# A post-norm transformer block: the transposed inputs of later batches made by DMAs and POOL, or by TensorE

## The chip, the core and the metric

The kernel runs on one core of one Trainium2 chip. The metric is the device time of one execution in microseconds (us). "Before" is the kernel as found; the profile of it is one further execution.

## The reference

Four batches of 512 tokens with 512 features go through attention (16 heads of 32, causal), a residual and a layer norm, then through a gated feed-forward layer with integer weights, a residual and a layer norm, all in float32. Cut to what matters:

```python
qkv = x @ w_qkv.T + b_qkv                    # x: (4, 512, 512), w_qkv: (1536, 512)
p = softmax(q @ k.T / sqrt(32) + causal)
x = layernorm(x + (p @ v) @ w_out.T + b_out)
g = x @ ((gate_w - 128) * gate_scale).T      # gate_w, up_w: (2048, 512), down_w: (512, 2048)
u = x @ ((up_w - 128) * up_scale).T
x = layernorm(x + (silu(g) * u) @ ((down_w - 128) * down_scale).T)
```

## The kernel before

**Engines and order.** Every engine's program is written out by hand and runs in its own order; semaphores join them. TensorE multiplies, ScalarE (ACT) and VectorE (DVE) empty the banks and split operands, GpSimd (POOL) and SyncE (SP) issue DMAs, and POOL does small vector work. An instruction that waits holds up all behind it on its engine.

**Attention.** The work goes in 16 groups: batch b has groups 4b to 4b+3, each with four heads. A group has 16 steps, and tables say what is done in which step: SCORE_STEPS, MAX_STEPS, EXP_STEPS, TASK_STEPS (transposes of probs through `ident`, L1296), and `filling`, which spreads projections between them. Every product of activations and weights is made of three matmuls from operands split into a high and a low part (xT_hi and xT_lo, wT_hi and wT_lo). The projections of group G+2 (L1220) stand in group G, so those of the next batch begin in step 8 of the group with g = 2.

**The transposed x.** A projection needs x with features on the partitions. Before, for batch b+1 SP loads x_tok (tokens on partitions, `load_x_ahead`, L518; y1 of batch 0 comes as the fourth such input, L521), TensorE transposes it in group 4b+2, steps 1, 2, 5 and 6 (X_STEPS; X_FIRST in group 2), four 128x128 transposes a step into one bank (`transpose_x`, L1192), ScalarE rounds the bank to xT_hi (`x_hi`, L750), and DVE takes the rest to xT_lo (`x_lo`, L952).

**Feed-forward.** Per batch 16 blocks i: `gate_up` makes 16 matmuls (L1438, L1439), ScalarE silu (L865), DVE hid (L1089), and `down` 8 matmuls (L1445, L1446). The weights are widened from shorter copies on the way: POOL's DMAs write 16-bit copies to DRAM during the attention (`shorten`), SP fetches them by transposing DMAs in four chunks (`load_short`, L545 to L551, 12 DMAs a chunk), and ScalarE widens them piece by piece in batch 0 (`widen_piece`, L828 and L833). If the weights' values didn't fit, a second path would read them through w_int instead; POOL issues the 48 loads of w_int (L722) in either case, each after the one two before it has landed. The input of batches 1 to 3 comes from y1_dram: SP loads x_tok, TensorE transposes it (L1405; in batch 0 as the last pieces of blocks 12 to 15, in batches 1 and 2 as turns between blocks, TURNS), ScalarE copies the banks to yT_next (L859, L922) and splits it (`y_hi`, L878), and DVE takes the low part (`y_lo`, L1098).

**POOL's order before.** Per group: `att_lo`, `widen_inverse` (a copy of 512 elements, L658), in some groups the layer norm's `apply_norm` (L645) and `add_bias`; after the attention the last `apply_norm`, then the 48 loads of w_int, then `root` for batches 0 to 2.

Of the kernel before, what the change touches and what calls it, by code (L numbers as in the profile page):

```python
# [6 lines left out]
def postln_block_kernel(nc: bass.Bass, x, w_qkv, b_qkv, w_out, b_out, gate_w, gate_scale, up_w, up_scale,  # L7
# [10 lines left out]
    BF16 = mybir.dt.bfloat16  # L18
# [49 lines left out]
    X_FIRST = [2, 4, 5, 6]  # L68
# [49 lines left out]
    def x_at(G, s):  # L118
        return [t for t in range(NT) if (X_STEPS if G > NG else X_FIRST)[t] == s] if G % NG == 2 else []

# [49 lines left out]
    for G, (jobs, counts) in enumerate(FILLING):  # L170
        for s in range(STEPS):
# [6 lines left out]
            for t in x_at(G, s):  # L178
                banks.whole(("x", G // NG + 1, t))
# [15 lines left out]
    down_short = nc.dram_tensor("down_short", (D, I), BF16, kind="Internal").ap()  # L195
    x_v = x.rearrange("b (t p) d -> b p t d", p=P)
# [14 lines left out]
    def pieces_at(i, short=False):  # L211
# [4 lines left out]
        if r == NI // TPR:  # L216
            return first + ahead + [("y", t)]
# [5 lines left out]
    WEIGHTS = [p for p in PIECES if p[0] != "y"]  # L223

    SHORT_PIECES = FIRST_PIECES + [p for i in range(NI) for p in pieces_at(i, True)]
    SHORT_WEIGHTS = [p for p in SHORT_PIECES if p[0] != "y"]
# [10 lines left out]
    TURNS = list(range(9)) + [("y", 0)] + list(range(9, 12)) + [("y", 2)] + list(range(12, NI))  # L237

# [5 lines left out]

    def of_batch(view, b):
        return view[bass.ds(b, 1)].rearrange("o p t d -> (o p) t d")

    ctx = ExitStack()
    with ctx:
# [9 lines left out]
        xT_hi = sb("xT_hi", [P, ND, S], F32R)  # L259
        xT_lo = sb("xT_lo", [P, ND, S], F32R)  # L260
# [104 lines left out]
        x_loaded = sem("x_loaded")  # L365
# [33 lines left out]
        yT_kept = sem("yT_kept")  # L399
        y_loaded = sem("y_loaded")  # L400
        r_loaded = sem("r_loaded")
        yT_full = sem("yT_full")
# [25 lines left out]
        def turns_of(ahead):  # L428
            return TURNS if ahead else list(range(NI))

        def piece_place(piece, weights):
# [7 lines left out]
            if kind == "d":  # L439
                return downT[:, TPR * n:TPR * (n + 1), piece[2] * P:(piece[2] + 1) * P]  # L440
            return yT_next[:, n, :].rearrange("p (t q) -> p t q", t=NT)
# [11 lines left out]
        def full_by(n, weights):  # L453

            return n + 1 if weights is wide_weights else sum(piece[0] == "y" for piece in PIECES[:n + 1])

        def piece_evicted(piece, order=WEIGHTS):

            if piece[0] == "y":
                return yT_kept, piece[1] + 1  # L460
            return fw_placed, order.index(piece) + 1
# [19 lines left out]
        def residual(b):  # L481
            return scan_buf if b == LAST else z_tok

# [3 lines left out]
        def _(sp):  # L487
# [25 lines left out]
            def load_x_ahead(b):  # L513

                for t in range(NT):
                    wait_full(sp, "x", b - 1, t)
# [1062 lines left out]
```

## Time and profile before

| | us |
|---|---|
| runs of the kernel before | 748.05, 748.51, 752.32 |
| median | 748.51 |
| the profiled execution | 748.73 |
| its span in the profile | 746.8 |
| TensorE busy | 724.9 (97%) |
| DVE, ScalarE, POOL busy | 393.5, 379.6, 135.4 |

The profile shows one execution. Matmuls overlap, so a line's mean duration is longer than the step from one start to the next; what a matmul costs in the queue is read from starts in the timeline. The first 383 us are the attention, the rest the feed-forward part, whose batches 1 and 2 take 88.8 us each.

### The profile page before, as it was taken

The page shows a single profiled execution, that of the slowest core. Times are in us where ns is not written, and L with a number is a line of the kernel's source. Part 1 is how long each engine was busy: PE and PEld are TensorE (multiplying, and loading weights), DVE is VectorE, ACT ScalarE, POOL GpSimd, SP SyncE. Part 2 cuts the span into 40 slices and gives each one's busy share as a digit, 9 for nine tenths or more (in the row PEclk, how much of TensorE's full clock was granted, in tenths as well). Part 3 has the DMA queues.
Part 4 walks back from the last instruction along what each step waited for, and adds up shares of the span by engine and source line. Part 5 has one row for each costly group of instructions (what it writes and reads, how often), then busy time and mean ns, then how long its engine had stood idle before and what let it go on. Part 6 is the DMA issues. An engine that isn't in the chain of part 4 may idle for free.

```text
span 746.8 us, 11957 instructions
## 1 busy us (share of the span) xinstructions
PE 724.9 (97%) x4480; PEld 564.2 (76%) x4480; DVE 393.5 (53%) x1004; ACT 379.6 (51%) x912; POOL 135.4 (18%) x154
## 2 busy tenths in 40 slices
PE   7998899999999999999899999999999999999994
PEld 6776677777777767777688888888888888888883
DVE  4766766666667665676652222643236332463335
ACT  3665866766866666866766554322232223322230
POOL 0010110305222151413724222220000000000004
PEclk9999999999999999999999999999999999999998
DMA  9201523335531465212577964431210020000201
GB/s 315 109 0 30 142 61 81 85 87 113 169 86 57 86 176 159 35 56 65 134 143 164 218 212 150 162 124 57 72 42 0 14 85 13 0 1 28 85 1 58
DMA packets 59463, 68.67 MB, mean 92 GB/s; under 512 B 33552, under 2 KB 35600, under 8 KB 59280
## 3 DMA queue, kind: packets, MB, share of 16 engines
q1 hardware_dynamic: 52880, 48.00, 21.8%
q0 software_dynamic: 6528, 19.93, 11.6%
q8 instruction: 35, 0.57, 0.3%
q14 instruction: 20, 0.16, 0.1%
HBM read 59.53 MB, written 14.68 MB: 99 GB/s over the span
## 4 chain that ended last, share of the span: by engine, by line
PE 92%; ACT 3%; DVE 2%; POOL 1%; DMA 1%; issue 0%; POOLq 0%; SPq 0%; DVEq 0%
PE bank L1438 16%; PE bank L1439 16%; PE bank L1220 12%; PE bank L1296 10%; PE bank L1445 7%; PE bank L1446 7%; PE bank L1235 6%; PE bank L1279 5%; PE bank L1317 5%; PE bank L1254 5%; ACT probs L757 2%; PE bank L1328 1%; DVE probs L973 1%; ACT xT_hi L750 1%; PE bank L1405 1%; PE bank L1182 1%
## 5 line engine op out<-in xcount | busy, mean ns | idle before, releaser
L757 ACT ACTIVATE probs<-probs,neg_max 128x128 f32<-128x128 f32 (+3 forms) x256 | 140.4, 553 | 4.3 <-DVE neg_max L973 4.2
L1089 DVE SCALAR_TENSOR_TENSOR hid<-bank,u_scale,silu 128x512 f32<-128x512 f32 x64 | 48.0, 750 | 164.3 <-PE bank L1439 163.1
L973 DVE CUSTOM_DVE_ANT_0 probs<-bank,causal 128x128 f32<-128x128 f32 (+3 forms) x256 | 111.6, 484 | 40.2 <-PE bank L1279 40.2
L1438 PE MATMUL bank<-xT_hi,gateT 128*128 128x512 f32 x256 | 100.3, 392 | 0.0
L1439 PE MATMUL bank<-xT_lo,gateT 128*128 128x512 f32 x256 | 99.7, 389 | 0.0
L1438 PE MATMUL bank<-xT_hi,upT 128*128 128x512 f32 x256 | 99.6, 389 | 0.0
L1439 PE MATMUL bank<-xT_lo,upT 128*128 128x512 f32 x256 | 99.6, 389 | 0.0
L1296 PEld LDWEIGHTS bank<-ident,probs 128*128 128x128 f32 x640 | 71.3, 141 | 35.9 <-issue 25.7
L809 ACT ACTIVATE probsT<-bank 128x512 f32<-128x512 f32 x80 | 47.7, 597 | 98.2 <-PE bank L1296 96.7
L865 ACT ACTIVATE silu<-bank,g_scale 128x512 f32<-128x512 f32 x64 | 44.0, 687 | 97.8 <-PE bank L1439 94.7
L871 ACT ACTIVATE hid_hi<-hid 128x512 fp32r<-128x512 f32 x58 | 36.7, 632 | 107.9 <-DVE hid L1089 107.9
L1296 PE MATMUL bank<-ident,probs 128*128 128x128 f32 x640 | 88.3, 277 | 2.4 <-DVE probsT L479 2.1
L1445 PE MATMUL bank<-downT,hid_hi 128*128 128x512 f32 x232 | 90.3, 389 | 0.1
L1446 PE MATMUL bank<-downT,hid_lo 128*128 128x512 f32 x232 | 90.3, 389 | 0.0
L479 DVE COPY probsT<-bank 128x512 f32<-128x512 f32 x80 | 54.8, 686 | 26.2 <-PE bank L1296 26.1
L1093 DVE TENSOR_TENSOR hid_lo<-hid,hid_hi 128x512 fp32r<-128x512 f32 x58 | 40.1, 692 | 40.5 <-ACT hid_hi L871 40.5
L1438 PEld LDWEIGHTS bank<-xT_hi,upT 128*128 128x128 f32 x256 | 48.1, 188 | 10.0
L1439 PEld LDWEIGHTS bank<-xT_lo,upT 128*128 128x128 f32 x256 | 48.0, 188 | 10.0
L1439 PEld LDWEIGHTS bank<-xT_lo,gateT 128*128 128x128 f32 x256 | 48.1, 188 | 9.8
L1438 PEld LDWEIGHTS bank<-xT_hi,gateT 128*128 128x128 f32 x256 | 48.1, 188 | 9.8
L1220 PE MATMUL bank<-xT_hi,wT_hi 128*128 128x512 f32 x128 | 54.4, 433 | 0.9 <-ACT probsT L809 0.8
L1445 PEld LDWEIGHTS bank<-downT,hid_hi 128*128 128x128 f32 x232 | 43.5, 188 | 9.3 <-issue 0.3
(102 smaller groups left out, 1158.8 us busy)
## 6 DMA issues: line engine op xcount, KB each, us to landing
scan_buf<-in_L_ffn_gate_w_dram SPq DMA_DIRECT2D x4, 1024.0 KB, 5.2
scan_buf<-in_L_ffn_up_w_dram SPq DMA_DIRECT2D x4, 1024.0 KB, 5.3
scan_buf<-in_L_ffn_down_w_dram SPq DMA_DIRECT2D x4, 1024.0 KB, 5.5
x_tok<-y_scratch SPq DMA_DIRECT2D x4, 1024.0 KB, 5.8
w_int<-in_L_ffn_gate_w_dram POOLq DMA_DIRECT2D x16, 256.0 KB, 3.3
w_int<-in_L_ffn_up_w_dram POOLq DMA_DIRECT2D x16, 256.0 KB, 3.0
w_int<-in_L_ffn_down_w_dram POOLq DMA_DIRECT2D x16, 256.0 KB, 3.7
z_tok<-y_scratch SPq DMA_DIRECT2D x4, 1024.0 KB, 5.6
```

What stands on the lines that cost most here:

```text
L479: copy(probsT[:, (G * BLOCKS + i) % SLOTS, :], bank_of("t", G, i)[:, :]).then_inc(drained_of("t", G, i), 1)
L757: nc.scalar.activation(probs[qb][:, j, :], probs[qb][:, j, :], ACT.Exp, bias=neg_max[:, qb, j:j + 1], scale=-1.0, accum_out=row_sum[:, qb, ...
L809: evict_task(act, G, i, lambda o, i: nc.scalar.activation(o, i, ACT.Copy))
L973: nc.vector.tensor_tensor_reduce(out=probs[qb][:, j, :], in0=score[j][:, first:first + w], in1=causal[:, S - w:S], scale=-SCALE, scalar=-F ...
L1089: nc.vector.scalar_tensor_tensor(out=hid[:, i % 2, :], in0=bank[:, :], scalar=u_scale[:, i:i + 1], in1=silu[:, i % 2, :], op0=ALU.mult, op ...
L1220: last = nc.tensor.matmul(acc[:, :], w[:, c, e], xT[:, c, :], start=at == 0, stop=at == MM - 1)
L1235: last = nc.tensor.matmul(acc[:, :], a[:, c, tok], w[:, c, 2 * D:3 * D], start=c == 0 and n == 0, stop=c == ND - 1 and n == 2)
L1296: last = nc.tensor.transpose(acc[:, m * P:(m + 1) * P], probs[qb][:, j, kb * P:(kb + 1) * P], ident[:, :])
L1438: nc.tensor.matmul(acc[n][:, :], w[:, c, cols], form(xT_hi[:, c, :]), start=c == 0, stop=False)
L1439: last = nc.tensor.matmul(acc[n][:, :], w[:, c, cols], form(xT_lo[:, c, :]), start=False, stop=c == ND - 1)
L1445: nc.tensor.matmul(down_acc[t][:, :], form(hi[:, tok]), w_down[:, i, :], start=i == 0, stop=False)
L1446: return nc.tensor.matmul(down_acc[t][:, :], form(lo[:, tok]), w_down[:, i, :], start=False, stop=i == NI - 1)
```

## The change

From the second input on, TensorE does not transpose. Each input (batches 1 to 3 of x, then y1 of batches 0 to 3) is taken as 1024 two-byte columns. `turn` has SP issue eight transposing DMAs into x_tok, `store_halves` writes the result to DRAM, `load_halves` reads it back so that the two halves of a float lie on one partition, 1 KB apart, and POOL's `join` interleaves them with four copies into x_whole (in xT_lo's place) or, in the feed-forward part, into yT_next. ScalarE and DVE then split from SBUF. The order lists X_STEPS and X_FIRST now hold chunks of features; the loops of SP and POOL over batches are written out.

```diff
+            def turn(n):
+
+                if n == 1:
+                    for t in range(NT):
+                        wait_full(sp, "x", 0, t)
                 else:
-                    sp.wait_ge(y1_stored, 16 * NT)
-                    sp.dma_start(x_tok[:, :, :], y1_v[0]).then_inc(x_loaded, 16)
-
-            load_x_ahead(1)
+                    sp.wait_ge(joined, ND * (n - 1))
+                if n == B + LAST - 1:
+                    sp.wait_ge(third_stored, 16 * NT)
+                elif n >= B:
+                    sp.wait_ge(y1_stored, 16 * NT * min(n - B + 1, LAST))
+                src = (x[n] if n < B else y1_dram[(n - B) * S:(n - B + 1) * S, :]).bitcast(U16)
+                for e in range(2 * ND):
+                    sp.dma_start(halves_turned[:, e, :], src[:, e * P:(e + 1) * P], transpose=True).then_inc(turned, 16)
+
+            def store_halves(n):
+                sp.wait_ge(turned, 16 * 2 * ND * n)
+                sp.dma_start(halves_dram[n].rearrange("(e p) s -> p e s", p=P), halves_turned).then_inc(halves_stored, 16)
+
+            def load_halves(n):
+                sp.wait_ge(halves_stored, 16 * n)
+                sp.dma_start(halves_short, halves_dram[n].rearrange("(c p h) s -> p c (h s)", p=P, h=2)).then_inc(halves_loaded, 16)
+
+            turn(1)
+            store_halves(1)
+            load_halves(1)
...
-                if g == 2 and b + 2 <= B:
-                    load_x_ahead(b + 2)
+                if g == 0 and b > 0:
+                    load_halves(b + 1)
+                if g == 2:
+                    turn(b + 2)
...
+                if g == 3:
+                    store_halves(b + 2)
...
-            for t in range(NT):
-                wait_full(sp, "x", B, t)
-            sp.dma_start(x_tok[:, :, :], y1_v[1]).then_inc(y_loaded, 16)
+            load_halves(B + 1)
             load_short(1)
...
             def ffn_batch(b, ahead):
                 if ahead:
-
-                    wait_alone(sp, yT_kept, b * ND)
-                    sp.dma_start(x_tok[:, :, :], of_batch(y1_v, b + 1)).then_inc(y_loaded, 16)
+                    turn(B + b + 1)
+                    store_halves(B + b + 1)
 
                 store_out(b - 1)
-                wait_alone(sp, out_stored, b * (16 * NT))
-                sp.dma_start(z_tok[:, :, :], of_batch(y1_v, b)).then_inc(r_loaded, 16)
-
-            with sp.Fori(1, B - 1) as b:
-                ffn_batch(b, True)
-            ffn_batch(B - 1, False)
+                sp.wait_ge(out_stored, b * (16 * NT))
+                sp.dma_start(z_tok[:, :, :], y1_v[b]).then_inc(r_loaded, 16)
+                if ahead:
+                    load_halves(B + b + 1)
+
+            for b in range(1, B):
+                ffn_batch(b, b < LAST)
             store_out(B - 1)
             sp.wait_ge(out_stored, 16 * B * NT)
...
+            def join(n):
+
+                pool.wait_ge(halves_loaded, 16 * n)
+                if n <= B:
+                    wait_full(pool, "k", NG * n - 1)
+                    out = x_whole
+                else:
+                    out = yT_next
+                    if n == B + 1:
+
+                        for kind in range(3):
+                            pool.wait_ge(staged[kind][2], 16 * ND)
+                    else:
+                        pool.wait_ge(yT_done, ND * (n - B - 1))
+                for c in range(ND):
+                    nc.gpsimd.tensor_copy(out[:, c, :].bitcast(U16).rearrange("p (s h) -> p s h", h=2),
+                                          halves[:, c, :, :].rearrange("p h s -> p s h")).then_inc(joined, 1)
+
...
             for G in range(GROUPS):
                 b, g = divmod(G, NG)
+                if g == 2:
+                    join(b + 1)
                 if G > 0:
                     att_lo(G - 1)
                 if g == 2 and b == LAST:
...
                 nc.gpsimd.dma_start(w_int[:, m % INTS, :], src).then_inc(fw_loaded[m % INTS], 16)
-            with pool.Fori(0, B - 1) as b:
+            join(B + 1)
+            for b in range(B - 1):
                 root(b, var2_done, rstd2_done)
+                if b + 2 < B:
+                    join(B + b + 2)
...
+            def next_hi(n, c):
+
+                act.wait_ge(joined, ND * (n - 1) + c + 1)
+                nc.scalar.activation(xT_hi[:, c, :], x_whole[:, c, :], ACT.Copy).then_inc(x_hi_done, 1)
...
-                act.wait_ge(yT_kept, b * ND + c + 1)
+                act.wait_ge(joined, b * ND + (ND * B + c + 1))
                 nc.scalar.activation(xT_hi[:, c, :], yT_next[:, c, :], ACT.Copy).then_inc(yT_hi_done, 1)
...
+            def next_lo(n, c):
+
+                dve.wait_ge(x_hi_done, NT + ND * (n - 1) + c + 1)
+                nc.vector.tensor_tensor(xT_lo[:, c, :], x_whole[:, c, :], xT_hi[:, c, :].bitcast(F32),
+                                        ALU.subtract).then_inc(xT_done, 1)
```

POOL's program from the last of the w_int loads on, before (w_int takes the raw weights, ln_rstd is `root`):

```order
L722 DMA w_int<-in_L_ffn_gate_w_dram 128x512 [waits fw_loaded0,fw_placed]
L722 DMA w_int<-in_L_ffn_up_w_dram 128x512 [waits fw_loaded1,fw_placed]
L723 UNCONDITIONAL_BRANCH
L723 ISA
L638 TENSOR_TENSOR ln_rstd<-ln_var,half_power 128x4 [waits var2_done]
L723 REGISTER_ALU
```

and changed:

```order
L752 DMA w_int<-in_L_ffn_gate_w_dram 128x512 [waits fw_loaded0,fw_placed]
L752 DMA w_int<-in_L_ffn_up_w_dram 128x512 [waits fw_loaded1,fw_placed]
L680 COPY yT_next<-x_tok 128x1024 [waits staged_u2,staged_d2,staged_g2,halves_loaded]
L680 COPY yT_next<-x_tok 128x1024 x3
L648 TENSOR_TENSOR ln_rstd<-ln_var,half_power 128x4 [waits var2_done]
L680 COPY yT_next<-x_tok 128x1024 [waits yT_done,halves_loaded]
L680 COPY yT_next<-x_tok 128x1024 x3
L648 TENSOR_TENSOR ln_rstd<-ln_var,half_power 128x4 [waits var2_done]
```

The four copies of each join stand between the loads and the roots, the first four behind all 48 loads.

SP's program from group 14 to the second chunk of short weights, before (stage takes the short weights, x_tok y1 of a batch):

```order
L545 DMA_TRANSPOSE stage<-gate_short 128x512 [waits short_ready0,work_full2]
L545 DMA_TRANSPOSE stage<-gate_short 128x512 x3
L548 DMA_TRANSPOSE stage<-up_short 128x512 x4
L551 DMA_TRANSPOSE stage<-down_short 128x512 x4
L577 DMA g_scale<-in_L_ffn_gate_scale_dram 128x16x1 [waits score_full2,score_full3,score_full1,score_full0]
L578 DMA u_scale<-in_L_ffn_up_scale_dram 128x16x1
L579 DMA d_scale<-in_L_ffn_down_scale_dram 128x512
L583 DMA x_tok<-y_scratch 128x4x512 [waits work_full0,work_full1,work_full2]
L545 DMA_TRANSPOSE stage<-gate_short 128x512 [waits short_ready1]
```

and changed:

```order
L519 DMA_TRANSPOSE x_tok<-y_scratch 128x512 [waits y1_stored,joined]
L519 DMA_TRANSPOSE x_tok<-y_scratch 128x512 x7
L553 DMA_TRANSPOSE stage<-gate_short 128x512 [waits short_ready0,work_full1]
L553 DMA_TRANSPOSE stage<-gate_short 128x512 x3
L556 DMA_TRANSPOSE stage<-up_short 128x512 x4
L559 DMA_TRANSPOSE stage<-down_short 128x512 x4
L523 DMA halves<-x_tok 128x8x512 [waits turned]
L589 DMA g_scale<-in_L_ffn_gate_scale_dram 128x16x1 [waits score_full2,score_full3,score_full1,score_full0]
L590 DMA u_scale<-in_L_ffn_up_scale_dram 128x16x1
L591 DMA d_scale<-in_L_ffn_down_scale_dram 128x512
L527 DMA x_tok<-halves 128x4x1024 [waits halves_stored]
L553 DMA_TRANSPOSE stage<-gate_short 128x512 [waits short_ready1]
```

The eight transposes of the next input stand ahead of the first chunk, and the store and the load of the halves ahead of the second.

TensorE's program in group 6, steps 0 to 2, before:

```order
L1254 MATMUL bank<-wT_hi,attT_hi 128x512 [waits work_drained1]
L1254 MATMUL bank<-wT_lo,attT_hi 128x512
L1254 MATMUL bank<-wT_hi,attT_lo 128x512
L1254 MATMUL bank<-wT_hi,attT_hi 128x512
L1192 MATMUL bank<-ident,x_tok 128x128 [waits work_drained2,x_loaded]
L1192 MATMUL bank<-ident,x_tok 128x128 x3
L1254 MATMUL bank<-wT_lo,attT_hi 128x512
L1254 MATMUL bank<-wT_hi,attT_lo 128x512
L1254 MATMUL bank<-wT_hi,attT_hi 128x512
L1254 MATMUL bank<-wT_lo,attT_hi 128x512
L1192 MATMUL bank<-ident,x_tok 128x128 [waits work_drained0]
L1192 MATMUL bank<-ident,x_tok 128x128 x3
```

and changed:

```order
L1281 MATMUL bank<-wT_hi,attT_hi 128x512 [waits work_drained2]
L1281 MATMUL bank<-wT_lo,attT_hi 128x512
L1281 MATMUL bank<-wT_hi,attT_lo 128x512
L1281 MATMUL bank<-wT_hi,attT_hi 128x512
L1281 MATMUL bank<-wT_lo,attT_hi 128x512
L1281 MATMUL bank<-wT_hi,attT_lo 128x512
L1281 MATMUL bank<-wT_hi,attT_hi 128x512
L1281 MATMUL bank<-wT_lo,attT_hi 128x512
```

The two sets of four transposes of x_tok are gone, and the eight matmuls around them follow one another.

## Rows read from the trace of the kernel before

**Rows 1.** The page's chain that ended last, by engine.
```profile
PE 92%; ACT 3%; DVE 2%; POOL 1%; DMA 1%; issue 0%; POOLq 0%; SPq 0%; DVEq 0%
```

**Rows 2.** Groups by line: transposes of x_tok (xcount, busy us, mean ns).
```profile
L1192 PE MATMUL bank<-ident,x_tok 128*128 128x128 f32 x80 | 13.1, 298 | 5.0 <-DMA x_tok<-in_L_attn_x_dram 4.0 <-DVE wT_lo L945 1.1
...
L1405 PE MATMUL bank<-ident,x_tok 128*128 128x128 f32 x48 | 6.5, 272 | 0.0
```

**Rows 3.** Timeline of TensorE, feed-forward batch 0 (start us, us, instruction).
```profile
457.75 0.39 PE L1446 MATMUL bank<-downT,hid_lo 128*128 128x512 f32 x1
457.98 0.60 PE L1405 MATMUL bank<-ident,x_tok 128*128 128x128 f32 x4
...
458.65 0.39 PE L1439 MATMUL bank<-xT_lo,gateT 128*128 128x512 f32 x1
...
473.76 0.39 PE L1438 MATMUL bank<-xT_hi,gateT 128*128 128x512 f32 x1
```

**Rows 4.** Timeline of POOL, its copies of inv_wide in groups 5, 7 and 8.
```profile
152.81 0.61 POOL L658 COPY inv_wide<-inv_sum 128x512 f32<-128x512 f32 x1 [6.82 <-DVE inv_sum L980]
...
198.89 0.61 POOL L658 COPY inv_wide<-inv_sum 128x512 f32<-128x512 f32 x1 [6.82 <-DVE inv_sum L980]
...
220.71 0.61 POOL L658 COPY inv_wide<-inv_sum 128x512 f32<-128x512 f32 x1 [6.81 <-DVE inv_sum L980]
```

**Rows 5.** Groups by line and shape, POOL's operations on 512 elements.
```profile
L645 POOL TENSOR_SCALAR z_tok<-z_tok,ln_mv,ln_rstd 128x512 f32<-128x512 f32 x16 | 33.5, 2101 | 0.8 <-POOL ln_rstd L638 0.7
...
L652 POOL TENSOR_TENSOR attT_lo<-attT,attT_hi 128x512 fp32r<-128x512 f32 x16 | 20.6, 1289 | 154.8 <-ACT attT_hi L771 154.8
...
L658 POOL COPY inv_wide<-inv_sum 128x512 f32<-128x512 f32 x16 | 9.8, 610 | 133.6 <-DVE inv_sum L980 133.6
```

**Rows 6.** Timelines of TensorE and ScalarE, groups 2 and 6.
```profile
75.83 0.39 PE L1220 MATMUL bank<-xT_lo,wT_hi 128*128 128x512 f32 x1
...
85.01 0.60 ACT L809 ACTIVATE probsT<-bank 128x512 f32<-128x512 f32 x1 [0.27 <-PE bank L1296]
...
159.41 0.40 PE L1220 MATMUL bank<-xT_lo,wT_hi 128*128 128x512 f32 x1
...
164.73 0.60 ACT L750 ACTIVATE xT_hi<-bank 128x512 fp32r<-128x512 f32 x1 [1.20 <-PE bank L1192]
...
172.40 0.59 ACT L750 ACTIVATE xT_hi<-bank 128x512 fp32r<-128x512 f32 x1
```

**Rows 7.** Timeline of POOL around its loads of w_int, and the tile's DMAs.
```profile
398.01 0.68 POOL L722 DMA_DIRECT2D w_int<-in_L_ffn_gate_w_dram  x1
...
479.54 0.54 POOL L722 DMA_DIRECT2D w_int<-in_L_ffn_down_w_dram  x1 [5.22 <-DMA w_int<-in_L_ffn_gate_w_dram]
...
498.60 1.06 POOL L638 TENSOR_TENSOR ln_rstd<-ln_var,half_power 128x4 f32<-128x4 f32 x1
...
DMA to landing us min/median/max: 2.6/3.5/6.1
```

**Rows 8.** Timelines of ScalarE and DVE, last split of the next batch's input.
```profile
471.70 0.63 ACT L878 ACTIVATE xT_hi<-yT_next 128x512 fp32r<-128x512 f32 x1
...
472.37 0.69 DVE L1098 TENSOR_TENSOR xT_lo<-yT_next,xT_hi 128x512 fp32r<-128x512 f32 x1 [0.21 <-ACT xT_hi L878]
```

**Rows 9.** Timelines of SP's transposing DMAs and ScalarE's down pieces.
```profile
352.05 6.11 SPq L545 DMA_TRANSPOSE stage<-gate_short  x4
...
375.79 6.80 SPq L545 DMA_TRANSPOSE stage<-gate_short  x4
...
398.58 1.32 ACT L828 ACTIVATE downT<-stage,minus_zero 128x512 fp32r<-128x512 bf16 x2
```

**Rows 10.** Granted clock (after the x counts) at the end; TensorE's first transposes.
```profile
741.00:744.00 3.00, 0.00 (x0) 0.00 (x0) 0.55 (x1) 0.00 (x0) 0.25 (x1) 0.63 0.46 175
...
3.66 1.09 PE L1192 MATMUL bank<-ident,x_tok 128*128 128x128 f32 x4 [3.66 <-DMA x_tok<-in_L_attn_x_dram]
...
5.92 2.49 PE L1192 MATMUL bank<-ident,x_tok 128*128 128x128 f32 x12 [0.32 <-DMA x_tok<-in_L_attn_x_dram]
```

More of the change, by code:

```diff
@@ L195, in postln_block_kernel @@
     down_short = nc.dram_tensor("down_short", (D, I), BF16, kind="Internal").ap()
+    halves_dram = [None] + [nc.dram_tensor(f"halves{n}", (2 * D, S), U16, kind="Internal").ap() for n in range(1, 2 * B)]
     x_v = x.rearrange("b (t p) d -> b p t d", p=P)
@@ L216, in pieces_at @@
         if r == NI // TPR:
-            return first + ahead + [("y", t)]
+            return first + ahead
         if short:
@@ L259, in postln_block_kernel @@
         xT_hi = sb("xT_hi", [P, ND, S], F32R)
+        whole = ExitStack()
+        x_whole = sb("x_whole", [P, ND, S], F32, whole)
+        whole.close()
         xT_lo = sb("xT_lo", [P, ND, S], F32R)
@@ L451, in hid_place, with piece_evicted @@
             return hid_hi[:, i % HIDS, :], hid_lo[:, i % HIDS, :]
[L453 to L460, printed above, removed]
+        def piece_evicted(piece, order=PIECES):
             return fw_placed, order.index(piece) + 1
@@ L482, in residual @@
             return scan_buf if b == LAST else z_tok
+        halves_turned = x_tok[:, :, :].bitcast(U16).rearrange("p c (e s) -> p (c e) s", e=2)
+        halves_short = x_tok[:, :, :].bitcast(U16)
+        halves = x_tok[:, :, :].bitcast(U16).rearrange("p c (h s) -> p c h s", h=2)
         block = ctx.enter_context(nc.Block())
@@ L1133, in ffn_batch @@
                 steps = finish(b - 1)
-                for n, i in enumerate(turns_of(ahead)):
-                    if not isinstance(i, tuple):
-                        hidden(b, i, up_acc[n % 2])
-                        next(steps, None)
+                for i in range(NI):
+                    hidden(b, i, up_acc[i % 2])
+                    next(steps, None)
                 if ahead:
@@ L1398, in ffn @@
                 short = weights is exact_weights
-                order = SHORT_WEIGHTS if short else WEIGHTS
-                def transpose_y(b, c, acc):
-                    if c == 0:
-                        pe.wait_ge(y_loaded, b * 16)
-                    for t in range(NT):
-                        last = nc.tensor.transpose(acc[:, t * P:(t + 1) * P], x_tok[:, t, c * P:(c + 1) * P], ident[:, :])
-                    return last
+                order = SHORT_PIECES if short else PIECES
                 def transpose_piece(n):
-                    piece = PIECES[n]
-                    if short and piece[0] != "y":
+                    if short:
                         return
@@ L1413, in transpose_piece @@
                         wait_at_rest(WORK + 2 + n)
-                    if n >= 2 and (not short or PIECES[n - 2][0] == "y"):
+                    if n >= 2:
                         pe.wait_ge(*piece_evicted(PIECES[n - 2], order))
                     acc = piece_bank[n % 2]
-                    if piece[0] == "y":
-                        transpose_y(1, piece[1], acc).then_inc(piece_full, 1)
-                        return
-                    m = WEIGHTS.index(piece)
-                    pe.wait_ge(fw_shifted, m + 1)
+                    pe.wait_ge(fw_shifted, n + 1)
                     for c in range(TPR):
-                        last = nc.tensor.transpose(acc[:, c * P:(c + 1) * P], w_shift[:, m % SHIFTS, c * P:(c + 1) * P],
+                        last = nc.tensor.transpose(acc[:, c * P:(c + 1) * P], w_shift[:, n % SHIFTS, c * P:(c + 1) * P],
                                                    ident[:, :])
@@ L1489, in ffn @@
                         pe.wait_ge(*piece_evicted(PIECES[n - 2]))
[L1490 removed]
+                    gate_up(0, i, first_bank(i), lambda c: pe.wait_ge(xT_done, ND * (B - 1) + c + 1))
                     if i == 1 and not short:
```

172 lines of the change are left out of this document (66 added, 106 removed).

## The prediction

> **What bounds the kernel now.** I read the page's chain first: TensorE carries 92% of it, ScalarE 3%, DVE 2%, DMA and POOL 1% each [rows 1]. So the end is set by how fast TensorE gets through its list, and removing work from it pays at once, as long as nothing new makes it wait. Next the groups by line: x goes through TensorE in 80 transposes of 128x128 at L1192 and 48 at L1405 [rows 2]. The first 16 of the 80 (batch 0) stay; 64 and 48 go. Then the timeline around one set of four, for its price in the queue, and last the queue of POOL, because the new work is put there and POOL does its list in order.
>
> **What goes from TensorE.** In the feed-forward part a matmul of 512 columns follows the one before it after 0.23 us. Around one set of four transposes, at 457.98, the matmul before starts at 457.75 and the second one after at 458.65 [rows 3]: 0.90 us, where two steps would be 0.45. Four transposes thus cost 0.45 us.
> - Feed-forward: 4 sets in batch 0 (1.8 us), 4 sets each in batches 1 and 2 (3.6 us).
> - Attention: 4 sets for each of 4 following inputs, 1.8 us by this price. From outside: POOL's inv_wide copy, one a group, stands at 152.81, then two groups on at 198.89, and one group on at 220.71 [rows 4]. The pair that holds the x transposes takes 46.08 us, twice 21.82 is 43.64: 2.4 us a batch. I take 2.0, so 8.0 in all, bounds 7.2 and 9.7.
> ScalarE's and DVE's splits of x (hi and lo) stay in number; only their input moves from a bank to SBUF. The twelve copies of yT out of the banks go, from engines that wait anyway; they count as nothing.
>
> **What comes to POOL.** join: four copies a batch of 1024 two-byte elements that interleave two halves lying 1 KB apart, 7 batches. No row shows such a copy. The nearest are POOL's own with 512 elements: COPY 610 ns, TENSOR_TENSOR 1289 ns, TENSOR_SCALAR 2101 ns [rows 5]. Doubled: 1.2, 2.6 and 4.2 us. I take 2.6, since the copy fetches from two places for each word that it writes, as TENSOR_TENSOR does, and keep 1.2 and 4.2 as ends.
> The Trainium skill ("GPSIMD Engine Reference", performance pitfalls for Q7 kernels) says that a read whose step exceeds 8 bytes costs about 2.9 cycles an element instead of 1.9. Its figure would make the copy an estimated 2.5 us; no run here shows it yet, and by the COPY row alone it would be 1.2. With the first the forecast below stays, with the second it is 5 to 7 us lower.
>
> **Is a join in time in the attention?** It waits until the last projection that reads xT_lo is done, because x_whole lies in its place. In group 6 that matmul starts at 159.41 and ends at 159.8; ScalarE splits x between 164.73 and 172.40 [rows 6]. Copies of 2.6 us are ready at 162.4, 165.0, 167.6 and 170.2; the four splits, moved up by the transposes that are gone, stand at about 164.3, 165.6, 169.2 and 170.7. All are met. Group 2 is tighter: its last projection starts at 75.83 (ends 76.2), so the fourth copy is ready at 86.6, and ScalarE takes the split in step 7, just ahead of the copy of probsT at 85.01 [rows 6], which TensorE wants. ScalarE waits about 2.3 us there and TensorE loses some 2. Attention: 8.0 - 2.0 = 6.0 us gained.
> The wait holds up ScalarE's in-order queue: exponentials behind it, and then TensorE's transposes of probs.
>
> **The join for feed-forward batch 1.** Here lies the cost. POOL first issues 48 loads of w_int, two in flight, each waiting for the one two before it to land. It issues them even on the path that reads the short weights, because the queue has no branch. The first starts at 398.01, POOL comes to the next kind of work only at 498.60, and a load takes 3.5 us to land in the median, 2.6 at least [rows 7]. The changed POOL queue has join(B+1) behind all of them. TensorE wants this input's last chunk at 473.76 [rows 3]. In today's kernel nothing on POOL was due by then. In the changed one:
> - loop's end 498.6, plus four copies 10.3, plus the last hi and lo: ScalarE starts at 471.70 and DVE's step starts at 472.37 and takes 0.69, together 1.4 [rows 8]. Ready: 510.3.
> - wanted: 473.76 less the 1.8 of batch 0's transposes: 472.0. Both sides shift alike by what the attention gains.
> - corrections to the loop: SP's load of x_tok from y_scratch for batch 2, 1 MB, is gone from its stretch; next to it POOL idled 5.22 us before the load at 479.54 [rows 7], against the two or so that a landing of 3.5 leaves with another load between: -3.0. The transposing DMAs of the short weights start some 10 us later (below) and overlap more of it: +1.3.
> - Wait: 510.3 - 472.0 - 1.7 = 36.6 us.
> TensorE waits here with nothing to do; down and gate_up behind it wait too, and ScalarE sits in y_hi.
>
> **Clock.** Once TensorE has stopped at the end of the run, its granted clock comes out at 0.63 over 741 to 744, with no matmul in the stretch [rows 10]: between the two levels, 2.4 and 1.2 GHz, so it fell in there. After 36 us without work TensorE will resume at 1.2 GHz. What a restart costs I read at the start of the run: four transposes take 1.09 us from 3.66 on and twelve 2.49 us from 5.92 on [rows 10], where four take 0.60 at 457.98 [rows 3] and twelve by that pace 1.5. With a set of weights between them, at the same pace, that is 0.5 + 0.5 + 1.0 = 2.0 us lost; bounds 0 and 4. The Trainium skill ("TensorE: Matmul & The Clock Gate", Part 1) has an idle array at 1.2 GHz and a busy one at 2.4; the 0.63 agrees.
>
> **SP's queue.** Eight transposing DMAs a batch, four take 6.1 to 6.8 us of SP [rows 9], so some 12 us. For most batches they fall between scans that have slack. In group 14 they stand ahead of load_short(0), which starts at 352.05 now; with copies of 2.6 us turn(5) begins near 350 and load_short(0) near 362. The scales and load_short(1), now at 375.79 [rows 9], come some 10 us later with it. ScalarE takes its first down piece of chunk 1 at 398.58 [rows 9], a couple of us after it lands today by an issue at 375.79 plus the 18 us of twelve such DMAs and 3 to 4 to land, and would wait about 8 us, TensorE 6 or so. That costs nothing in the sum: it lies inside the 36.6 us for which TensorE waits anyway, since POOL's loop does not depend on it. Without that wait it would be paid in full. The later joins have a whole batch of 87 us: SP transposes at once, stores, waits for the outputs and reloads some 50 us in.
>
> **Sum,** against the profiled execution, 748.7 (span 746.8 and 1.9 around it), which is within 0.2 us of the median 748.5:
> 748.7 - 6.0 (attention) - 1.8 - 3.6 (feed-forward) + 36.6 + 2.0 = 775.9 us, 3.7% slower.
>
> **Rivals.**
> 1. Fast copies, 1.2 us. For: the COPY row. Against: it reads one dense or repeated stream. The wait shrinks by 5.4, group 2 loses nothing: 768.5; with attention at 9.7 and no clock loss 764.8.
> 2. Slow copies, 4.2 us. Group 6's are ready at 164.0, 168.2, 172.4, 176.6; ScalarE waits some 6 us a batch, TensorE 4 to 5; group 2 is late by 8.8 at the fourth, TensorE 7 or so. Attention then loses 5 x 3 + 7 = 22 less the 8 gained; the last wait grows by 6.5: 748.7 + 14 - 5.4 + 43.1 + 2 = 802. For: two-byte elements at two steps may run far from the dense rate; against: TENSOR_SCALAR does two arithmetic operations.
> 3. Faster: the w_int loop ends in time, and the 112 transposes are simply saved: 748.7 - 8.0 - 5.4 = 735.3, or 741 with SP's delay. It decides at the loop's length: with 1.2 us copies it must be done within about 67 us (472 less 1.4 and 4.9, less 398), 1.4 us a load instead of 2.1. Even at the least landing of 2.6 us and 0.54 to issue, two in flight give 1.57 [rows 7]. Nearly ruled out.
> 4. The transposes saved are filled by other waits in attention (gain 2 or less): about 780.
>
> **Chances.** The forecast with its neighbour 4 (770 to 782) 0.57, rival 1 0.2, rival 2 0.18, rival 3 0.03, and 0.02 for a time within 1%. About 1% is what a measurement of this kernel tells from no change. Range: 764 takes in rival 1, 792 a good half of the way to rival 2. Faster 0.03, same 0.02, slower 0.95.
>
> **What would show it.** One idle stretch of TensorE of 30 to 40 us between feed-forward batches 0 and 1, released by ScalarE or DVE on xT, these by POOL's copy, that by the last w_int load, which still comes near 100 us after the first. Attention groups with x at 22.5 us or so. join's mean between 1.2 and 4.2 us. Wrong if the loop is much shorter than 90 us, if TensorE idles elsewhere for over 5 us in sum, or if join's mean lies outside its bounds.

## The result and the profile after

| | before | after |
|---|---|---|
| median, us | 748.65 (4 runs, 748.05 to 752.32) | 772.75 (4 runs, 770.71 to 772.96) |
| the profiled execution, us | 748.73 | 770.71 |
| its span, us | 746.8 | 768.6 |
| TensorE's mean granted clock in it | 0.997 | 0.977 |

The ratio is 1.0305, 95% interval 1.0268 to 1.0342: slower by 3%. The 775.9 us predicted lie some 3 us above the median, and the range of 764 to 792 holds it. The terms below show how much of that agreement was luck.

The page of the changed kernel: totals, TensorE's busy tenths and clock in 40 slices, and the chain by engine, as [rows 1].

```profile
PE 715.2 (93%) x4368; PEld 554.5 (72%) x4368; DVE 398.3 (52%) x1004; ACT 374.6 (49%) x900; POOL 167.9 (22%) x182
...
PE   7998899999999999997999993299999999999995
...
PEclk9999999999999999999999997599999999999998
...
PE 84%; DVE 6%; DMA 4%; ACT 3%; issue 1%; POOL 1%; SPq 0%; POOLq 0%; DVEq 0%; ACTq 0%
```

TensorE's share of the chain fell from 92% to 84%, and it is busy for 9.7 us less (715.2 against 724.9). Two slices (24 and 25, about 460 to 500 us) have it nearly idle, and its clock is down in the same ones. The page's chain gives each engine's share of what ended last. Who TensorE waited for (sum, times, longest one):

```profile
PE bank L1451 <- DVE xT_lo L1127: 27.5, 1, 27.5
PE bank L1323 <- DVE probsT L467: 5.3, 6, 1.8
...
PE bank L1306 <- DVE neg_max L1002: 3.2, 2, 2.2
```

One wait of 27.5 us. The releaser named is DVE, but DVE is only the last link. A window inside the wait (TensorE, its weight loads, DVE, ScalarE and POOL busy, then the granted clock, the DMA share and GB/s):

```profile
480.00:490.00 10.00, 0.00 (x0) 0.00 (x0) 0.00 (x0) 0.00 (x0) 3.02 (x6) 0.50 0.53 156
```

TensorE's timeline, first matmul of the feed-forward part and then both ends of the wait:

```profile
379.76 0.39 PE L1451 MATMUL bank<-xT_hi,gateT 128*128 128x512 f32 x1
...
467.36 0.40 PE L1459 MATMUL bank<-downT,hid_lo 128*128 128x512 f32 x1
495.21 0.79 PE L1451 MATMUL bank<-xT_hi,gateT 128*128 128x512 f32 x1 [27.45 <-DVE xT_lo L1127]
495.80 0.63 PE L1452 MATMUL bank<-xT_lo,gateT 128*128 128x512 f32 x1
...
500.49 0.43 PE L1451 MATMUL bank<-xT_hi,upT 128*128 128x512 f32 x1
500.76 0.39 PE L1452 MATMUL bank<-xT_lo,upT 128*128 128x512 f32 x1
```

The kernel before has the matching two places (first matmul of the feed-forward part, first of its batch 1) here:

```profile
383.13 0.39 PE L1438 MATMUL bank<-xT_hi,gateT 128*128 128x512 f32 x1
...
472.40 0.39 PE L1438 MATMUL bank<-xT_hi,gateT 128*128 128x512 f32 x1
```

The timelines of three engines in the changed kernel lead the wait back to its root, as [rows 7, 8]. POOL:

```profile
394.62 0.68 POOL L752 DMA_DIRECT2D w_int<-in_L_ffn_gate_w_dram  x1
...
489.66 0.54 POOL L752 DMA_DIRECT2D w_int<-in_L_ffn_up_w_dram  x1 [1.35 <-DMA w_int<-in_L_ffn_up_w_dram]
490.19 4.41 POOL L680 COPY yT_next<-x_tok 128x1024 uint16<-128x1024 uint16 x4
```

ScalarE:

```profile
491.44 0.63 ACT L909 ACTIVATE xT_hi<-yT_next 128x512 fp32r<-128x512 f32 x1 [26.65 <-POOL yT_next L680]
```

DVE:

```profile
492.10 3.05 DVE L1127 TENSOR_TENSOR xT_lo<-yT_next,xT_hi 128x512 fp32r<-128x512 f32 x1 [26.58 <-ACT xT_hi L909]
```

The 48 loads take POOL from 394.62 to 490.19, the join starts at once behind them, and TensorE resumes at 495.21. What it waits for there is the low part of the first of the four chunks, not of the last: ScalarE had that chunk's high part at 492.07, and DVE's subtraction, 0.68 us elsewhere, took 3.05 us, until just after POOL's fourth copy ended at 494.60. TensorE resumes at half clock: 12 matmuls from 495.21 to 500.49 take 5.28 us, where by the step of batch 1's first matmuls in the kernel before (472.40 to 473.76, six steps [rows 3]: 0.227) they would take 2.7.

Later batches are shorter. SP's stores of the output, four per batch, start in the changed kernel at:

```profile
529.67 16.65 SPq L613 DMA_DIRECT2D out_dram<-z_tok  x4
...
616.71 16.65 SPq L613 DMA_DIRECT2D out_dram<-z_tok  x4
```

And in the kernel before:

```profile
504.43 16.66 SPq L603 DMA_DIRECT2D out_dram<-z_tok  x4
...
593.29 16.66 SPq L603 DMA_DIRECT2D out_dram<-z_tok  x4
```

Read the first pair against the second: 87.04 us a batch instead of 88.86, so 1.8 for batch 1; batch 2 goes the same way (87.04 against 88.72, from the next stores at 703.75 and 682.01).

**Where the 21.8 us of span come from** (768.6 - 746.8):
- attention: 379.76 against 383.13, -3.4;
- batch 0 up to the first matmul of batch 1: 467.76 - 379.76 = 88.0 against 472.40 - 383.13 = 89.3, -1.3;
- the wait, +27.45;
- the half clock, 5.28 - 2.72, +2.56;
- batches 1 and 2, -3.5 (87.04 twice against 88.86 and 88.72).

Their sum is +21.8.

### The profile page after: what moved, and what is told of

The parts are those of the page before. It is cut to its first block, busy times and chain, and to the rows that moved or that the text cites. A ratio compares the mean times of both kernels' runs of the same rounds, so it can differ in the third digit from the quotient of the medians.

```text
span 768.6 us, 11736 instructions
## 1 busy us (share of the span) xinstructions
PE 715.2 (93%) x4368; PEld 554.5 (72%) x4368; DVE 398.3 (52%) x1004; ACT 374.6 (49%) x900; POOL 167.9 (22%) x182
## 4 chain that ended last, share of the span: by engine, by line
PE 84%; DVE 6%; DMA 4%; ACT 3%; issue 1%; POOL 1%; SPq 0%; POOLq 0%; DVEq 0%; ACTq 0%
PE bank L1451 15%; PE bank L1452 15%; PE bank L1244 11%; PE bank L1323 9%; PE bank L1459 7%; PE bank L1458 7%; PE bank L1262 6%; PE bank L1306 5%; PE bank L1344 5%; PE bank L1281 4%; DVE probs L1002 2%; ACT probs L795 2%; DMA w_int<-in_L_ffn_up_w_dram 2%; DMA w_int<-in_L_ffn_down_w_dram 1%; DVE xT_lo L981 1%
## 5 line engine op out<-in xcount | busy, mean ns | idle before, releaser
L1451 PE MATMUL bank<-xT_hi,gateT 128*128 128x512 f32 x256 | 100.7, 393 | 27.5 <-DVE xT_lo L1127 27.5
L1306 PE MATMUL bank<-k_sb,q_sb 32*128 32x512 f32 (+3 forms) x512 | 48.1, 467 | 3.3 <-DVE neg_max L1002 3.2
```

The costliest lines, as they stand in the source:

```text
L1306: last = nc.tensor.matmul(score[j][:, first:first + w], q_sb[G % 2][rows, qb * P:(qb + 1) * P], k_sb[G % 2][rows, 0:w], start=True, stop=True)
L1451: nc.tensor.matmul(acc[n][:, :], w[:, c, cols], form(xT_hi[:, c, :]), start=c == 0, stop=False)
```

## The experiments

**1. a_skip: the loads of w_int only on the path that needs them.** In the changed kernel POOL takes the 48 loads under the branch that ScalarE and TensorE already have; the join keeps a place in the middle of batch 0.

```diff
+            pool.wait_ge(scan_done, 1)
+            wide = pool.value_load(wide_flag[0:1, 0:1], min_val=0, max_val=1)
+            with pool.If(wide > 0):
                 for m in range(len(PIECES)):
...
+            pool.wait_ge(*piece_evicted(PIECES[36]))
             join(B + 1)
```

> The changed kernel with the same branch: no loads of w_int ahead of the join for feed-forward batch 1, which waits instead for the 37th piece of weights to be placed. Theory (TensorE's 27.5 us of idle time and the half clock after it come from the loads ahead of that join): idle stretch gone, 770.7 - 27.5 - 2.6 = 740.6 us, 1% faster than the kernel before. Rival (the path over DRAM or the copies are late by themselves): TensorE still waits 5 us or more there, 748 us or above.

Measured: 740.23 us median (739.17 to 741.37), 0.987 of before (0.9839 to 0.9901). POOL's timeline:

```profile
395.25 2.07 POOL L655 TENSOR_SCALAR z_tok<-z_tok,ln_mv,ln_rstd 128x512 f32<-128x512 f32 x1
440.90 4.47 POOL L680 COPY yT_next<-x_tok 128x1024 uint16<-128x1024 uint16 x4 [43.58 <-ACT gateT L875]
```

No wait of TensorE for xT is left in the feed-forward part. The change as such is a gain; the loads ahead of the join in POOL's queue turn it into a loss. This is the experiment that decides.

The 740.6 of the theory is met within 0.4 us, but partly by luck. Besides the wait and the half clock, 2.5 us at the very end are gone with the loads (experiment 2), and the attention of this profile took 2.6 us more than the changed kernel's (feed-forward part from 382.39 instead of 379.76), mostly because the clock fell in it.

**2. b_skip: the same branch in the kernel before.** This is the control of the first: does taking the loads away help by itself?

```diff
+            pool.wait_ge(scan_done, 1)
+            wide = pool.value_load(wide_flag[0:1, 0:1], min_val=0, max_val=1)
+            with pool.If(wide > 0):
                 for m in range(len(WEIGHTS)):
```

> The kernel before, with POOL's 48 loads of w_int left out on the path that reads the short weights (a branch on the flag that ScalarE and TensorE branch on too). Theory (the loads cost nothing there, since nothing on POOL is due before they end): 748.5 us, within 0.5. Rival (their DMA traffic or POOL's lateness with the first root costs the kernel before something too): 2 us or more faster.

Measured: 746.45 us median (746.17 to 749.51) against 749.16, ratio 0.997 (0.9948 to 0.9992). The theory's half microsecond is missed, by about 2 us, and the rival's number, 2 us or more, is the one that came. But neither of the rival's reasons is seen: from the first matmul of the feed-forward part to DVE's last row both profiles take 358.16 us (383.13 to 741.29, 386.33 to 744.49). The difference stands at the very end. DVE's last row in the kernel before:

```profile
741.29 0.55 DVE L1000 TENSOR_SCALAR z_tok<-z_tok,ln_mv,ln_rstd 128x512 f32<-128x512 f32 x1 [0.44 <-POOL ln_rstd L728]
```

b_skip:

```profile
744.49 0.55 DVE L1003 TENSOR_SCALAR z_tok<-z_tok,ln_mv,ln_rstd 128x512 f32<-128x512 f32 x1 [0.44 <-POOL ln_rstd L731]
```

The spans are 746.8 and 747.5: 5.0 us after the end of that row with the loads, 2.5 without. It is so in all nine profiles: 4.9 to 5.0 in the five with the loads, 2.4 to 2.5 in the four without. What happens in those 2.5 us the trace doesn't name; no run here tests it. So of the 8.9 us between a_skip and before, some 2.5 belong to the missing loads and not to the transposes: against b_skip, a_skip is 6.2 us faster (740.23 and 746.45).

The profile of b_skip ends later than that of the kernel before, although the median is lower. Its seven times fall in two groups, four of 746.17 to 746.45 and three of 749.0 to 749.51, and the profiled one (749.47) is of the second. In it the first inv_wide copy is already 1.7 us late (40.60 against 38.94), and the clock fell in group 14, where nothing differs from the kernel before:

```profile
360.00:364.00 4.00, 4.00 (x36) 3.06 (x40) 1.20 (x3) 2.21 (x7) 3.81 (x3) 0.61 0.46 102
```

**3. a_mid: the join ahead of the 39th load.** Nothing is taken away; only the place in POOL's queue differs.

```diff
             for m in range(len(PIECES)):
...
+                if m == 38:
+                    join(B + 1)
                 kind, n = PIECES[m][:2]
...
-            join(B + 1)
```

> The changed kernel with that join put ahead of the 39th of the 48 loads, where POOL comes 17 us earlier. Theory: TensorE's wait shrinks by just these 17 us to about 10, the clock still falls in it, 770.7 - 17.2 = 753.5 us. Rival (the loads' own landing sets it, so moving the join in the queue does little): above 760 us.

Measured: 757.92 us median (755.9 to 759.15), ratio 1.0097 (1.0065 to 1.0129): 14.8 us of the 24 given back by the place alone. POOL's row of the join,

```profile
479.18 5.36 POOL L680 COPY yT_next<-x_tok 128x1024 uint16<-128x1024 uint16 x4 [0.85 <-DMA w_int<-in_L_ffn_up_w_dram]
```

and TensorE's waits for the low part (sum, times, longest):

```profile
PE bank L1452 <- DVE xT_lo L1128: 13.2, 3, 12.5
```

The wait follows the join: it starts 11.0 us earlier (479.18 against 490.19), and the wait is 14.3 us less. The other 3.3 us have two sources. Batch 0 ended 1.7 us later here (last matmul at 469.10 against 467.36), and the first low part was there 2.8 us after the join's start (matmul at 482.02) instead of 5.0, since DVE was not held up until the last copy; two short waits of 0.3 us for later chunks come on top. My 753.5 put the join at 473; POOL reached it 6 us later, and the clock fell here too (0.50 in 475 to 485), although the wait was half as long.

**4. a_twice2: each join copy made twice.** A dose of the copy's price, the output unchanged.

```diff
+                    view = out[:, c, :].bitcast(U16).rearrange("p (s h) -> p s h", h=2)
+                    nc.gpsimd.tensor_copy(view, halves[:, c, :, :].rearrange("p h s -> p s h")).then_inc(once, 1)
+                    pool.wait_ge(once, ND * (n - 1) + c + 1)
+                    nc.gpsimd.tensor_copy(view, halves[:, c, :, :].rearrange("p h s -> p s h")).then_inc(joined, 1)
```

> The changed kernel with every join copy made twice, the second after the first (output unchanged). Theory (the wait between feed-forward batches 0 and 1 is the end of POOL's w_int loop plus the four copies plus the last splits; copies are 1.1 us each): the join of that batch takes 9.0 instead of 4.5 us, the wait of TensorE grows from 27.5 to 32 us, and group 2, where the join is tightest, loses 1 to 2 us more: 775.5 to 779 us, 3.6 to 4.0% over the kernel before. Rival A (attention's joins are all tight, DVE and ScalarE wait for each): the joins of groups 6, 10 and 14 cost 1 us or more each too, 781 us or more. Rival B (the copies are hidden and the loop alone counts): 773 us, no change to the changed kernel.

Measured: 788.03 us median (785.87 to 789.27), ratio 1.0517 (1.0499 to 1.0535), far over all that the theory allowed. TensorE's timeline in group 2, where the longest wait of the changed kernel was 2.19 us (below):

```profile
89.84 1.43 PE L1326 MATMUL bank<-ident,probs 128*128 128x128 f32 x8 [3.00 <-DVE probsT L468]
```

The window behind it (TensorE, its weight loads, DVE, ScalarE and POOL busy, then the granted clock, the DMA share and GB/s):

```profile
85.00:95.00 10.00, 7.00 (x28) 5.25 (x27) 6.25 (x23) 5.64 (x18) 3.82 (x5) 0.73 0.60 106
```

The feed-forward part starts at 387.89, 8.1 us later than in the changed kernel. By POOL's inv_wide copies group 2 grew by 4.2 us, the group after it by 1.5 (its clock had fallen), groups 6 and 10 by 0.7 each, group 14 by 1.2. So the attention is tight against a copy of 2.3 us. Rival A had the direction, my theory hadn't, but of the groups 6, 10 and 14 only the last reached the 1 us that the rival asked of each.

In the feed-forward part the loads took 1.7 us more, TensorE's first matmul on the fourth chunk came another 4.0 us later, and the low clock behind the wait lasted 1.3 us more. Together 15.1 us with the attention's 8.1, and the profiled spans differ by 15.2. TensorE's wait for the low parts did not grow to the theory's 32 us; it is 27.4 (four waits, the longest 23.3), because batch 0 itself took 4.8 us more (92.8 instead of 88.0). SP came late with the short weights there: ScalarE waited 4.7 us for a down piece at 408.16, TensorE 3.0 us behind it at 410.97, and the clock fell once more (0.83 in 410 to 420). All that lies inside the wait for the join.

**5. a_near: the join reads only the upper half of each word,** and writes it to both halves of the result (x and y1 are thus altered). The reads go in steps of 0 and 2 bytes, with no jump of 1 KB.

```diff
-                                          halves[:, c, :, :].rearrange("p h s -> p s h")).then_inc(joined, 1)
+                                          halves[:, c, 1, :].unsqueeze(2).broadcast_to((P, S, 2))).then_inc(joined, 1)
```

> The changed kernel, with the join copies reading only the upper two-byte half of each word, each value written to both halves of the result: same 1024 two-byte elements written per copy, but the source is read at steps of 0 and 2 bytes instead of jumping 1 KB (the low half of every x is thus a copy of the high half, the output differs). Theory (a copy on POOL costs about 1.1 ns a two-byte element whatever the step): mean of one stays 1.10 to 1.15 us, the time stays 772.5 within 1.5 us. Rival (the page's rule that a read step over 8 bytes costs 2.9 instead of 1.9 cycles): the near read takes two thirds, 0.75 us, and the wait between the batches shrinks by 1.5 us, to 26.

Measured: 770.86 us, in one run. The copies in the feed-forward part, min/median/max ns, in the changed kernel:

```profile
L680 POOL COPY yT_next<-x_tok x12: 1141/1153/1164, 490.2 to 646.7; 128x1024 uint16<-128x1024 uint16 x12
```

In a_near:

```profile
L680 POOL COPY yT_next<-x_tok x12: 1033/1038/1048, 491.5 to 646.8; 128x1024 uint16<-128x1024 uint16 x12
```

Near reads are 10% cheaper, neither unchanged as I expected nor a third cheaper. (The rule weighed is that of the Trainium skill, "GPSIMD Engine Reference", performance pitfalls for Q7 kernels, which has a read step above 8 bytes at about 2.9 cycles an element instead of 1.9; the measurement speaks against it for this copy.) The copy costs about 1.1 ns an element, and little of it goes by the step. TensorE's wait came out at 26.3 us, near the rival's 26, but not by its reason: the copies account for 0.4 us of the difference, and the rest is that batch 0 ended 2.0 us later while the loads ended only 1.3 us later.

This run showed something else. Its attention ends 2.0 us later than the changed kernel's in its profile (381.80 against 379.76) with the same waits of TensorE there. Two windows of 4 us each, in group 14, of the changed kernel (the clock is the third number from the end):

```profile
352.00:356.00 4.00, 2.28 (x19) 2.05 (x20) 3.41 (x16) 3.16 (x13) 2.24 (x3) 1.00 0.44 98
356.00:360.00 4.00, 3.87 (x52) 2.21 (x49) 1.85 (x7) 2.08 (x8) 3.99 (x3) 1.00 0.62 104
```

And of a_near:

```profile
352.00:356.00 4.00, 2.98 (x18) 2.74 (x19) 2.56 (x12) 2.70 (x9) 3.03 (x3) 0.65 0.44 98
356.00:360.00 4.00, 4.00 (x40) 1.91 (x39) 0.78 (x2) 1.34 (x5) 3.99 (x3) 0.50 0.51 105
```

After some 5 us of waits for DVE the clock stayed in one execution and halved in the other. a_near's mean clock is 0.974 against 0.977. The three other runs of the changed kernel stand at 0.972 to 0.974 too, so they may have this loss. But they are 2 us longer than the profiled one, and a_near, at 770.86, is not: quicker loads (0.7 us), quicker copies (0.4) and a shorter stretch of half clock (0.7) gave it back all but 0.2 us. The three were not profiled, and what made them longer stays open.

**6. s_poollo: POOL computes the attention's low parts of x, instead of DVE,** on top of a_skip.

```diff
+                if g == 2:
+                    for c in range(ND):
+                        pool.wait_ge(x_hi_done, NT + ND * b + c + 1)
+                        nc.gpsimd.tensor_tensor(xT_lo[:, c, :], x_whole[:, c, :], xT_hi[:, c, :].bitcast(F32),
+                                                ALU.subtract).then_inc(xT_done, 1)
...
-                        next_lo(b + 1, c)
```

The reason for it lies in group 6. The window of 160 to 176 us (columns as above) of the kernel before:

```profile
160.00:176.00 16.00, 15.83 (x144) 11.15 (x137) 12.44 (x37) 10.52 (x27) 1.28 (x1) 1.00 0.39 131
```

Of the changed kernel:

```profile
160.00:176.00 16.00, 15.18 (x121) 10.50 (x113) 13.89 (x47) 12.51 (x35) 5.17 (x6) 1.00 0.51 117
```

Of s_poollo:

```profile
160.00:176.00 16.00, 16.00 (x118) 12.00 (x115) 13.64 (x47) 14.12 (x40) 11.85 (x12) 1.00 0.51 97
```

With the transposes gone TensorE is less busy than before, not further on: it waits for DVE, which has its list pushed closer together. Two of these waits in the changed kernel, in groups 2 and 6:

```profile
81.97 0.94 PE L1306 MATMUL bank<-k_sb,q_sb 32*128 32x128 f32 x16 [2.19 <-DVE neg_max L1002]
...
174.64 1.09 PE L1323 MATMUL bank<-ident,probs 128*128 128x128 f32 x8 [0.79 <-DVE probsT L467]
```

> The version without the w_int loop (a_skip), with attention's four low parts of x per batch computed by POOL (right behind its join and att_lo) instead of DVE. Theory (the attention gained 3.4 us instead of 8 since in the groups that hold x DVE, busy without a gap over steps 0 to 8, takes over as the bound once the transposes are gone): with 0.7 to 0.9 us x 4 off DVE in each of four groups the waits of TensorE for DVE's probsT and neg_max shrink and the feed-forward part starts 2 to 5 us earlier than the 380 us of a_skip, the time falls from 740.2 to 735 to 738.5 us (1.4 to 1.8% under the kernel before). Rival A (POOL's 1.3 us subtractions or their port get in the way of DVE): no gain or a loss, 740 to 743. Rival B (ScalarE or the order of TensorE's own work bounds these groups): DVE gets idle time, TensorE's waits stay, 740 us.

Measured: 736.03 us median (735.38 to 737.06), ratio 0.9823 (0.9809 to 0.9837), the fastest of all; a_skip had 0.987. TensorE is busy for the whole 16 us. POOL's inv_wide copies at both ends of group 6, in the changed kernel:

```profile
151.85 0.61 POOL L686 COPY inv_wide<-inv_sum 128x512 f32<-128x512 f32 x1 [6.82 <-DVE inv_sum L1009]
...
175.51 0.61 POOL L686 COPY inv_wide<-inv_sum 128x512 f32<-128x512 f32 x1 [7.66 <-DVE inv_sum L1009]
```

In s_poollo:

```profile
150.70 0.61 POOL L686 COPY inv_wide<-inv_sum 128x512 f32<-128x512 f32 x1 [6.82 <-DVE inv_sum L1018]
...
172.52 0.61 POOL L686 COPY inv_wide<-inv_sum 128x512 f32<-128x512 f32 x1 [0.76 <-DVE inv_sum L1018]
```

Group 6 takes 21.82 us, exactly a group without an x, where the changed kernel has 23.66; the two groups behind it are together 0.6 us shorter in the changed kernel, so the low parts on DVE cost it 1.3 us net, and as much in group 10. The theory holds for these two groups: DVE was the bound there. In group 2 only 0.2 us are won, and in group 14 POOL's longer row costs 1.2 (25.85 against 24.68). The feed-forward part starts at 377.38, 5.0 us ahead of a_skip's, but 1.9 us of that are the clock, which fell in a_skip's group 2 and not here, and 1.0 is an earlier start of the whole.

**7. s_mixed: as s_poollo, but with DVE's low parts in group 14,** where TensorE had waited 1.9 us for POOL.

```diff
-                if g == 2:
+                if g == 2 and b < LAST:
```

> The previous version (s_poollo: no w_int loop, attention's low parts on POOL) but with the last group that holds an x, group 14, as in a_skip: there DVE computes them. In s_poollo POOL had copies, four subtractions and add_bias of the last batch in a row in that group, and TensorE waited 1.9 us for its inv_wide copy. Theory (POOL's row is the cause): that wait goes, TensorE's waits for probsT and neg_max in group 14 return to those of a_skip (4 us in all, against 2.6 + 1.9), the time is 734.5 to 736.5 us, at most 1 us better than 736.0. Rival (DVE's part is worth more than POOL's row costs): 737 us or more.

Measured: 737.74 us median (737.55 to 737.85), ratio 0.9847 (0.9829 to 0.9864). The rival's number holds, its reason is not what shows. As the theory had it, group 14 is shorter with DVE's low parts, 24.70 us against 25.85 by the inv_wide copies. But the next one takes 18.33 against 15.78: TensorE's waits in group 14 add up to 4.9 us (probsT, z_tok, neg_max) instead of 4.5, and the clock behind them was down for longer. As the clock's fall differs between executions, this pair doesn't settle which engine should have the low parts there. In s_poollo:

```profile
352.00:356.00 4.00, 4.00 (x44) 1.95 (x42) 0.00 (x0) 0.60 (x1) 3.81 (x3) 0.60 0.61 101
```

And in s_mixed:

```profile
352.00:356.00 4.00, 4.00 (x28) 2.97 (x32) 1.23 (x3) 2.23 (x7) 3.81 (x3) 0.50 0.46 103
356.00:360.00 4.00, 3.76 (x40) 1.89 (x32) 1.25 (x5) 0.64 (x2) 4.00 (x3) 0.78 0.63 94
```

## Why the prediction was right, and where it wasn't

| term | predicted | profiled |
|---|---|---|
| attention | -6.0 | -3.4 |
| feed-forward batch 0 | -1.8 | -1.3 |
| batches 1 and 2 | -3.6 | -3.5 |
| the wait for the join | +36.6 | +27.45 |
| clock after it | +2.0 | +2.56 |
| sum on 748.7 | 775.9 | 770.5 (the execution: 770.71) |

**The mechanism is shown.** The single idle stretch, its place, and its chain (TensorE, the splits, the copies, the last load of w_int) are in the trace as forecast, and moving the join past the loads (a_mid) or removing them (a_skip) moves or removes the wait. The loop's 95.6 us are 3.3 less than the 98.9 that I had after corrections.

**The copy was mis-sized.** The failed step is "I take 2.6, since the copy fetches from two places for each word that it writes, as TENSOR_TENSOR does". It measures 1.15 us. The COPY row doubled, 1.2, was the right neighbour: same operation, twice the elements. Four copies take 4.4 us instead of 10.3, and 36.6 - 5.9 - 3.3 = 27.4 is the wait as found. That it fits to a tenth is chance: the sum counts up to the fourth chunk's low part, and TensorE waited for the first one's, which came just after the fourth copy's end (495.15 and 494.60). The estimate from the Trainium skill ("GPSIMD Engine Reference", performance pitfalls for Q7 kernels), 2.5 us for a read step above 8 bytes, isn't borne out either: 1.15 us with steps of 1 KB against 1.04 with steps of 0 and 2 bytes (a_near). Rival 1 had this price, and with 768.5 it was below the result because it kept all 8 us of gain in the attention (3.4 came); its wait of 31.2 was 3.7 too long and hid most of that.

**The attention's gain was mis-sized twice, and the errors hid each other.** "ScalarE's and DVE's splits of x stay in number" is true, and it was my reason to charge nothing for them; but DVE's work in those groups then has some 2 us less to fit into, and DVE becomes the bound. s_poollo shows it for groups 6 and 10. By the inv_wide copies the x batches gained 1.35, 1.2, 1.1 and 0.1 us in groups 2, 6, 10 and 14 (with the group or two behind each), not 2.0; why group 14 gained next to nothing stays open, as neither s_poollo nor s_mixed gives it back. For the price of 2.6 us I took all joins to be in time but group 2's, and charged 2.0 us. a_twice2 has copies near that price, and its feed-forward part starts 4.8 us later than in the kernel before (387.89 against 383.13), not 6 earlier. Had the copies cost 2.6 us, the kernel would have run at about 788 (an estimate from a_twice2's 788.03 with copies of 2.3), and my 775.9 would have been 12 too low. As it was, the wait was priced 9.2 us too high (5.9 for the copies, 3.3 for the loop) and all else 3.8 too low, which leaves 5.4 against the profiled execution; that the other runs took 2 us more than that one brought the median nearer still. The overpriced copy and the underpriced attention partly cancelled: a number near the result doesn't vouch for its terms.

**SP's lateness didn't come.** I had load_short(0) at 362 and load_short(1) some 10 us late. SP's timeline:

```profile
340.43 10.27 SPq L519 DMA_TRANSPOSE x_tok<-y_scratch  x8
350.79 5.12 SPq L553 DMA_TRANSPOSE stage<-gate_short  x4
...
375.97 4.23 SPq L553 DMA_TRANSPOSE stage<-gate_short  x3
```

The last turn began 10 us earlier than thought, some 6 of them because the join ahead of it is fast (four copies in 4.46 us), and load_short(1) is where it was (375.79 in [rows 9]). With slow copies it comes as forecast: in a_twice2 the last turn began at 352.55 and load_short(1) at 387.29, ScalarE waited 4.7 us for its down piece where I had 8, batch 0 took 4.8 us more where I had 6, and it hid in the wait for the join.

**Clock.** That it falls in the wait and what the return costs came out as worked from [rows 10], 2.56 us against 2.0. The Trainium skill ("TensorE: Matmul & The Clock Gate", Part 1) has an idle array at 1.2 GHz; the 0.50 of the idle stretch agrees. Left out was that the clock can fall in the attention as well, behind waits of 1 to 3 us each; the next group was 0.5 to 2.8 us longer each time (0.5 in a_skip's group 15, 2.8 in a_near's).

## What to carry to other kernels

Work taken off the bounding engine is worth what the next wait leaves of it. Before counting it, look at what else stands in the same stretch on the engines that feed it, and at the whole queue ahead of each new step, dead work included: 48 loads that nothing reads cost 2.5 us at the end of the kernel before, and over 27 once something useful stood behind them. To price an operation that no row shows, take the row of the same operation and scale it by elements before one that merely resembles it; here that was right within 5%.

## What the runs showed of the hardware

- DVE's subtractions and POOL's copies, both on SBUF tiles, slow each other when they overlap. DVE's xT_lo at 492.10 took 3.05 us, until just after POOL's copies ended at 494.60; the other three took 0.68. In a_mid the four copies took 5.36 us beside DVE instead of 4.41. In a_skip's join of group 2 DVE's subtractions reached 1.66 us.
- The clock's fall after short waits is not the same in every execution: with nearly equal waits in group 14 it stayed at 1.00 in one profile and fell to 0.50 in another. It fell in the attention in all seven profiles of the experiments, and in neither of those of the kernel before and the changed one. One of the seven is b_skip, whose attention is that of the kernel before. Part of the spread of the kernel before (748.05 to 752.32) may be this.
- With the loads of w_int issued, the span ends 5.0 us after DVE's last instruction (five profiles), without them 2.5 (four). The cause stays open.
